# A three-pass product of rounded halves in a fused decoder layer's cross attention

## What is computed

```
q = l @ Wq;  k, v = split(concat([x, l]) @ Wkv)       # l: latents, x: context, both normalized
w = softmax(q k^T / 8)                                # 64 queries, 128 keys, 16 heads
out = (w @ v) @ Wo
```

## Time and profile before

| | us |
|---|---|
| median of 3 runs | 1611.88 (1607.72 to 1613.25) |
| the profiled execution, its own time | 1606.26 |
| its span | 1604.4 |
| PE busy in the span | 1432.5 (89%) |
| DVE busy | 1105.5 (69%) |
| ACT busy | 1031.7 (64%) |
| POOL busy | 904.7 (56%) |

### The profile page before, as it was taken

How to read it: one execution, slowest core, us unless ns; L and a number is a source line. 1 busy time by engine, 2 the same in 40 slices (tenths; PEclk the granted TensorE clock), 3 DMA queues, 4 the chain that set the end, 5 groups by cost and what they waited for, 6 DMA issues and landing times.

```text
span 1604.4 us, 36488 instructions
## 1 busy us (share of the span) xinstructions
PE 1432.5 (89%) x10509; PEld 1239.7 (77%) x10509; DVE 1105.5 (69%) x4107; ACT 1031.7 (64%) x3827; POOL 904.7 (56%) x1233
## 2 busy tenths in 40 slices
PE   5699999999999999999999999999997499999940
PEld 4578888888888888888888888888886498889940
DVE  3366777767777677776777767777666588777865
ACT  2377776777767777677776777767764255555535
POOL 3355556665566665666556665566544255455565
PEclk9799999999999999999999999999999699999975
DMA  2000000000000000000000000000000676677746
GB/s 78 11 11 8 15 16 15 18 16 15 16 15 18 17 14 16 15 18 17 14 16 15 17 17 14 16 16 17 10 10 14 181 242 218 213 221 225 222 153 196
DMA packets 64624, 96.18 MB, mean 60 GB/s; under 512 B 10892, under 2 KB 48786, under 8 KB 64306
## 3 DMA queue, kind: packets, MB, share of 16 engines
q1 hardware_dynamic: 44738, 71.90, 15.0%
q0 software_dynamic: 8896, 16.94, 3.1%
q10 hardware_dynamic: 10800, 5.06, 1.2%
HBM read 71.55 MB, written 23.35 MB: 59 GB/s over the span
## 4 chain that ended last, share of the span: by engine, by line
PE 69%; DVE 10%; ACT 9%; DMA 4%; issue 4%; POOL 2%; SPq 2%; ACTq 0%; POOLq 0%; DVEq 0%
PE ps_s L1208 15%; PE ps_o L1221 11%; PE ps_t L1241 10%; ACT probs L607 6%; PE ps_pT L1231 5%; PE ps_t L1371 3%; PE ps_u L1256 3%; PE ps_a L1307 3%; PE ps_u L1258 3%; PE ps_u L1257 3%; DVE neg_max L759 3%; DVE pT L771 3%; PE ps_u L1371 2%; DVE k_pick L814 2%; DMA f_x<-x_rows 2%
## 5 line engine op out<-in xcount | busy, mean ns | idle before, releaser
L607 ACT ACTIVATE probs<-ps_s,neg_max 128x128 f32<-128x128 f32 x1024 | 361.8, 366 | 290.2 <-DVE neg_max L759 290.2
L496 POOL TENSOR_TENSOR probs_n<-probs,inv_sum 128x512 f32<-128x512 f32 x256 | 265.9, 1039 | 251.6 <-DVE inv_sum L765 249.6
L1208 PE MATMUL ps_s<-kvT,u_sb 128*128 128x128 f32 x2048 | 281.1, 280 | 0.0
L1208 PEld LDWEIGHTS ps_s<-kvT,u_sb 128*128 128x128 f32 x2048 | 255.2, 192 | 33.2 <-issue 31.8
L1241 PE MATMUL ps_t<-pT,kv_rows 128*128 128x512 f32 x512 | 262.2, 594 | 0.8 <-DVE pT L771 0.8
L1221 PE MATMUL ps_o<-value_w,tT 128*128 128x128 f32 x2048 | 260.5, 275 | 2.4 <-ACT tT L618 2.2
L759 DVE TENSOR_REDUCE neg_max<-ps_s 128x4 f32<-128x512 f32 x256 | 176.2, 688 | 103.9 <-PE ps_s L1208 103.4
L1221 PEld LDWEIGHTS ps_o<-value_w,tT 128*128 128x128 f32 x2048 | 244.0, 192 | 4.3 <-ACT tT L618 4.3
L553 POOL DMA_INDIRECT y_rows<-wvT,f_id x144 | 144.8, 1006 | 152.4 <-DVE wvT L1118 94.9
L607 ACT ACTIVATION_READ_ACCUMULATOR probs<-ps_s,neg_max 128x1 f32 x1024 | 208.2, 203 | 0.0
L508 POOL DMA_INDIRECT x_rows<-routed,pos_i x128 | 136.7, 1068 | 121.2 <-DVE pos_i L950 101.0
(11 more groups left out here) (237 smaller groups left out, 3165.6 us busy)
## 6 DMA issues: line engine op xcount, KB each, us to landing
u_sb<-in_expert_w SPq DMA_DIRECT2D x45, 578.0 KB
tT<-in_expert_w SPq DMA_DIRECT2D x27, 578.0 KB
f_x<-x_rows SPq DMA_DIRECT2D x72, 130.0 KB
tT<-y_rows SPq DMA_DIRECT2D x16, 512.0 KB, 4.7
x_raw<-in_x SPq DMA_DIRECT2D x64, 64.0 KB, 1.8
c_raw<-in_ctx_in SPq DMA_DIRECT2D x64, 64.0 KB, 2.0
out<-u_sb ACTq DMA_DIRECT2D x16, 256.0 KB, 2.4
y_rows<-wvT,f_id POOLq DMA_INDIRECT x144
```

The costliest lines, as they stand in the source:

```text
L496: nc.gpsimd.tensor_tensor(probs_n[:, sl], probs[:, sl], inv_sum[:, sl, :].rearrange("p (u o) -> p u o", o=1).to_broadcast([P, UP, P]), ALU ...
L607: last = nc.scalar.activation(probs[:, sl, j], ps_s[sl][:, j * P:(j + 1) * P], ACT.Exp, bias=neg_max[:, sl, j:j + 1], accum_out=sums[:, sl ...
L1208: last = nc.tensor.matmul(ps_s[sl][:, j * P:(j + 1) * P], u_sb[:, c // 2, BT * p + b, h:h + 2].rearrange("p h s -> p (h s)"), kvT[:, c, 2 ...
```

## The change

The product of key rows and transposed probabilities becomes three matmuls of float32r operands, `hi*hi + lo*hi + hi*lo`, accumulated in `ps_t`. ACT's copy L670 writes `kv_hi`, and a new DVE operation `rows_low` writes `kv_lo`, the rest. `keep_pT` is split in two: `round_pT` stands where it stood and writes the high part, and a new `keep_pT`, some operations later on DVE, subtracts the high part from the bank and writes the rest.

```
-        kv_rows = sb("kv_rows", [P, KV_RING, BT, D])
+        kv_hi = sb("kv_hi", [P, KV_RING, BT, D], F32R)
+        kv_lo = sb("kv_lo", [P, KV_RING, BT, D], F32R)
-        pT = sb("pT", [P, 2, UP * P])
+        pT_hi = sb("pT_hi", [P, 2, UP * P], F32R)
+        pT_lo = sb("pT_lo", [P, 2, UP * P], F32R)
...
-                        nc.scalar.activation(kv_rows[:, (t + 2) % KV_RING], KV_BACK.rearrange("p (b d) -> p b d", b=BT),
-                                             ACT.Copy).then_inc(kv_done, 1)
+                        nc.scalar.activation(kv_hi[:, (t + 2) % KV_RING], KV_BACK.rearrange("p (b d) -> p b d", b=BT),
+                                             ACT.Copy).then_inc(kv_hi_done, 1)
...
-                def keep_pT(k):
+                def round_pT(k):
                     m, ss = t * 4 + (k - 1), (k - 1) % 2
                     dve.wait_ge(pT_ps, m + 1)
                     dve.wait_ge(t_ps, count(m - 1))
-                    nc.vector.tensor_copy(pT[:, ss], ps_pT[:]).then_inc(pT_done, 1)
+                    nc.vector.tensor_copy(pT_hi[:, ss], ps_pT[:]).then_inc(pT_hi_done, 1)
+
+                def keep_pT(k):
+                    m, ss = t * 4 + (k - 1), (k - 1) % 2
+                    dve.wait_ge(pT_hi_done, m + 1)
+                    nc.vector.tensor_tensor(pT_lo[:, ss], ps_pT[:], pT_hi[:, ss].bitcast(F32), ALU.subtract).then_inc(pT_lo_done, 1)
...
+                def rows_low():
+                    dve.wait_ge(kv_hi_done, t + 3)
+                    nc.vector.tensor_tensor(kv_lo[:, (t + 2) % KV_RING], KV_BACK.rearrange("p (b d) -> p b d", b=BT),
+                                            kv_hi[:, (t + 2) % KV_RING].bitcast(F32), ALU.subtract).then_inc(kv_lo_done, 1)
```

```
             def turn_probs(t, k):
                 m, ss = t * 4 + (k - 1), (k - 1) % 2
                 pe.wait_ge(p_done, m + 1)
-                pe.wait_ge(pT_done, m)
+                pe.wait_ge(pT_lo_done, m)
...
-                pe.wait_ge(pT_done, m + 1)
-                pe.wait_ge(kv_done, m // 4 + 1)
+                own = m // 4 % KV_RING
+                pe.wait_ge(pT_hi_done, m + 1)
+                pe.wait_ge(kv_lo_done, m // 4 + 1)
                 pe.wait_ge(t_done, m)
-                nc.tensor.matmul(ps_t[:], kv_rows[:, m // 4 % KV_RING, b], pT[:, ss], start=True, stop=True).then_inc(t_ps, 1)
+                nc.tensor.matmul(ps_t[:], kv_hi[:, own, b], pT_hi[:, ss], start=True, stop=False)
+                nc.tensor.matmul(ps_t[:], kv_lo[:, own, b], pT_hi[:, ss], start=False, stop=False)
+                pe.wait_ge(pT_lo_done, m + 1)
+                nc.tensor.matmul(ps_t[:], kv_hi[:, own, b], pT_lo[:, ss], start=False, stop=True).then_inc(t_ps, 1)
```

More of the change, by code:

```diff
@@ L271, in decoder_layer @@
         neg_top_done g_lat_set kv_ps z1_done z1_stats z1_moments z1_eps z1_rstd x1_done l_hat_done
-        kv_done kvT_ps kvT_done lT_done upper_done score_split u_ps u_done s_ps max_done exp_done inv_done p_done pT_ps pT_done
+        kv_hi_done kv_lo_done kvT_ps kvT_done lT_done upper_done score_split u_ps u_done s_ps max_done exp_done inv_done p_done pT_ps pT_hi_done pT_lo_done
         t_ps t_done o_ps z2_done z2_stats z2_moments z2_eps z2_rstd x2_done
@@ L280, in decoder_layer @@
          neg_top_done, g_lat_set, kv_ps, z1_done, z1_stats, z1_moments, z1_eps, z1_rstd, x1_done, l_hat_done,
[L281 to L282 removed]
+         kv_hi_done, kv_lo_done, kvT_ps, kvT_done, lT_done, upper_done, score_split, u_ps, u_done, s_ps, max_done, exp_done, inv_done,
+         p_done, pT_ps, pT_hi_done, pT_lo_done, t_ps, t_done, o_ps, z2_done, z2_stats, z2_moments, z2_eps, z2_rstd,
          x2_done, x2T_ps, x2T_done, gate_ps, logits_done, gexp_done,
@@ L973, in period @@
                 if unit_on(t, -1):
-                    keep_pT(0)
+                    round_pT(0)
                 if on(t, -4):
@@ L984, in period @@
                     z1_mean()
+                if unit_on(t, -1):
+                    keep_pT(0)
                 if isinstance(t, int) and t == FIRST:
@@ L1001, in period @@
                 if unit_on(t, 0):
-                    keep_pT(1)
+                    round_pT(1)
                 if on(up, 2):
                     x1_norm()
+                if unit_on(t, 0):
+                    keep_pT(1)
+                if on(t, 2):
+                    rows_low()
                 if isinstance(t, int) and t == FIRST:
@@ L1015, in period @@
                 if unit_on(t, 1):
-                    keep_pT(2)
+                    round_pT(2)
                 if on(t, -4):
                     place_all()
+                if unit_on(t, 1):
+                    keep_pT(2)
                 if isinstance(t, int) and t == FIRST:
@@ L1037, in period @@
                 if unit_on(t, 2):
-                    keep_pT(3)
+                    round_pT(3)
                 if on(up, 3):
@@ L1041, in period @@
                     kv_product()
+                if unit_on(t, 2):
+                    keep_pT(3)
                 if on(t, -4):
@@ L1296, in period @@
                         pe.wait_ge(logits_done, min(t - 2, NT))
-                        pe.wait_ge(kv_done, min(t + 3, NT))
+                        pe.wait_ge(kv_lo_done, min(t + 3, NT))
                         nc.tensor.matmul(B_RANK, ones[:], seen[:, p], start=True, stop=False)
```

## The result

The changed kernel takes 1659.86 us in the median (1652.47 to 1663.43, 4 runs), the one before 1609.8 beside it: ratio 1.032, 95% interval 1.029 to 1.035, so it is slower by 3%. Its profiled execution has a span of 1654.9 us, 50.5 above the 1604.4 of before.

A forecast was written before the change was run, and what follows sets the result against it. DVE's order of operations was taken to bound the changed kernel: +0.89 us a period over 55 periods, 49, plus 6 elsewhere, takes 1606.3 to 1661; as a median, 5.6 higher, 1667, range 1640 to 1705.

The forecast's parts named there:

- R1 and R2: Starts of row_max(1) and row_max(2) in a period; claimed set by DVE's own order, with no idle ahead.
- The size of an addition: DVE time a 512-element keep_pT subtraction occupies: 0.59 us taken, 0.69 the upper bound.
- The first three: Stretches between starts of row_max(0) to row_max(3): forecast 5.52, 4.49 and 3.65 us.
- The last: Stretch from row_max(3) to the next row_max(0), with keep_pT(3) behind kv_product: 5.45 us, between 5.31 and 5.59.
- 6 us to the nine other periods: Periods with fewer DVE operations, between 0 and 0.9 us each; 6 in all with run-in and tail.
- TensorE's part: weigh on PE: three passes of 0.224 us make 0.67 against 0.86, saving 0.19 a unit (0.14 to 0.21).
- PE's stall in unit 1: PE idles 0.7 us ahead of turn_probs(1), waiting for keep_pT(0); parallel to DVE's work, adding nothing.
- R0 to R3: From row_max(0)'s start to row_max(3)'s: 13.66 us needed on DVE, about 12.34 on PE.
- The margin of 0.06: In unit 1, rows_low would start 0.06 us after ACT's copy of the key rows ends, so that wait costs nothing.
- the first: Rival: DVE's idle time hides its additions and PE's saving is booked, 1576 us as a median; chance 0.07.
- POOL and DVE do block each other: Rival: blocking or a late key-row copy adds 0.6 to 1.0 us a period, 1700 to 1722; chance 0.17.
- The clock: Rival: PE's clock falls as PE idles more, about +290 us, 1900; chance 0.03.

The follow-up runs named there:

- the passes alone: Changed kernel without VectorE's subtractions, low parts zeros written once, turn_probs waiting for the copy as before: 1569.01 us, 0.982 of the kernel before.
- the run with the wait alone: Kernel before, with turn_probs waiting for a two-element maximum on VectorE in each of keep_pT's new places: 1629.73 us, ratio 1.012.
- the run of DVE's part alone: Changed kernel with one float32 product as before; all of DVE's additions and the wait of turn_probs kept, subtraction results unused: 1658.26 us, 1.036 of before.
- The run with ScalarE's extra copy: Changed kernel with ScalarE writing the probabilities' high part right after its unit's exponentials, VectorE the low part alone: 1645.75 us, 1.029 of the kernel before.
- six placements of the same subtractions: Changed kernel (1.032), and five with its keep_pT or rows_low operations moved on VectorE: 1.096, 1.013, 1.007, 1.015 and 0.988 of the kernel before.

## Why the prediction was right

- **The bound.** The reading that R1 and R2 were already set by DVE, though the chain of waits put those stretches on PE, carried the forecast. The additions on DVE alone give 1.036, the passes alone 0.982.
- **The size of an addition.** 0.59 was taken, with 0.69 as the other bound, and 0.60 was measured: the follower of the subtraction at 858.36 starts at 858.96. The record is 0.68 long in the mean, as the rows near it had it. The rule of the Trainium skill that the prediction weighed (VectorE: DVE Perf Modes, The DRAIN you can't avoid) would have given 0.4 a period more, and no segment shows it. The same section adds that an operation which is not held starts earlier, without a size; that sentence is the one that fits the 0.60, and the prediction left it out.
- **The segments.** The first three came out within 0.02. (For R2 to R3 the two terms named add to 3.68, 3.09 and 0.59, and not to 3.65; 3.66 was measured.) The last was mis-sized: 5.45 forecast, 5.36 measured, 0.09 too much, 5 us over 55 periods: 44 for the full periods against 49 forecast. The bounds were "between 5.31 (all absorbed) and 5.59", and most of `keep_pT(3)` was absorbed. That it was by the wait ahead of `scale_queries`, as the prediction named it, is read from the trace of before and was not tried.
- **The rest.** I gave 6 us to the nine other periods, the run-in and the tail; it is 7.0 for the nine periods, less 4.1 and plus 3.5 for the ends, 6.4 in all. That the total fits is luck: the two ends nearly cancel, and the prediction had no terms for them.
- **TensorE's part.** 0.224 was taken for a pass and 0.23 measured, so a unit gains 0.17, not 0.19. That PE's stall in unit 1 (0.7 forecast, 0.86 measured) would be parallel to DVE's work held in the changed kernel, but by little. The forecast set DVE's 13.66 from R0 to R3 against 12.34 for PE and called PE no longer near the bound. It left its own 0.7 of stall out of the 12.34, and it did not price the restart behind a wait, 0.37 a period in the run with the wait alone, where TensorE binds. In the changed kernel `score(3)` ends 13.51 behind `score(0)` in the mean, and `row_max(3)` starts 0.26 behind it. That DVE and not PE sets R3 came true with 0.2 to spare and not 1.3; without the passes it would not have (3.76 in the run of DVE's part alone). PE is 91% busy where 89% was forecast.
- **`rows_low` and ACT.** The margin of 0.06 was there (858.90 against 858.96). The run with ScalarE's extra copy shows what was behind it: 1.2 us a period.
- **The rivals.** The limit of the first, 1.66, should be the 1.63 of idle time that it names; an operation of 0.33 us follows either way, and 0.60 was measured. POOL and DVE do block each other, but the change didn't add to it: the additions themselves are not blocked, and the held operations took as long as before (764 ns for the first of `route_rows` against 757, 675 for `x1_norm` in both). The clock stayed at 1.00 from 300 to 500 us with PE 91% busy. The forecast treated 0.59 as the cost wherever an operation stands behind `inverse_sum`; that holds for the places in the change, not in general: directly behind `round_pT(0)` it cost 0.11.

The forecast median of 1667 is 7 us above the 1659.86 measured: 5 from the last segment, and the before kernel's own median was 1609.8 in the new comparison, 2 below the one used.

## What to carry to other kernels

Write down for each engine where its own order, and not its input, sets the next step, and price an addition there, not against its idle share. Before moving an operation into idle time, list who waits for its result and what shares its bank: over six placements of the same subtractions (one with `x1_norm` moved too) the time went from 0.988 to 1.096 of the kernel before. An operation that is held up by another engine marks a place for work that is not: the subtraction put ahead of one cost 0.11 us there in place of 0.58.

## What the runs showed of the hardware that was not expected

- Four transposes behind a wait start 0.14 to 0.15 us after the VectorE operation that releases them (855.02 behind 854.88 in the changed kernel, 411.66 behind 411.51 in the run with the wait alone), and count 0.63 us in the chain, against 0.44 where they follow other work, whose end their record overlaps by 0.16.
- A VectorE scalar operation and a copy of two elements a row took 0.79 and 1.05 us while GpSimd multiplied, and 0.22 and 0.15 otherwise, while a subtraction of 512 elements with one operand in PSUM took 0.69 beside the multiplication and 0.66 to 0.69 elsewhere.
